# Banded attention of one layer: the softmax division moved from the weights to the output, with its sums on TensorE

## The reference, cut to what matters

```
def _pointwise(W, b, t):
    return jnp.einsum('oc,bct->bot', W, t) + b[None, :, None]
q, k, v = _pointwise(Wq, bq, x), _pointwise(Wk, bk, cond), _pointwise(Wv, bv, cond)
k, v = padded by 8 on the left and 7 on the right
k_win = k[:, :, idx].reshape(B, H, hd, T, W)
v_win = v[:, :, idx].reshape(B, H, hd, T, W)
dots = jnp.einsum('bhdt,bhdtw->bhtw', qh, k_win) * scale
attn = jax.nn.softmax(dots, axis=-1)
out = jnp.einsum('bhtw,bhdtw->bhdt', attn, v_win)
return _pointwise(Wo, bo, out.reshape(B, C, T))
```

## Time and profile before

| what | value |
|---|---|
| median of 3 runs | 2366.32 us (2362.61 to 2378.12) |
| the profiled execution, its own time | 2366.56 us |
| its span, first to last instruction | 2364.5 us |
| TensorE busy | 1939.2 us (82%) |
| VectorE busy | 1702.7 us (72%) |
| ScalarE busy | 559.1 us (24%) |
| GpSimd busy | 609.7 us (26%) |
| mean granted clock of TensorE | 0.894 |

### The profile page before, as it was taken

One profiled execution on the slowest core, in us unless ns is written; L12 is line 12 of the kernel. 1 busy time (PEld: TensorE's weight loads), 2 busy tenths in 40 slices (PEclk: granted clock), 3 DMA queues, 4 the chain that ended last, 5 costly groups with the idle time before them and its releaser, 6 DMA issues. The chain is left out here.

```text
span 2364.5 us, 40599 instructions
## 1 busy us (share of the span) xinstructions
PE 1939.2 (82%) x14722; PEld 1103.0 (47%) x14872; DVE 1702.7 (72%) x3005; ACT 559.1 (24%) x1326; POOL 609.7 (26%) x728
## 2 busy tenths in 40 slices
PE   4587879877898788887766798989899989898876
PEld 2343556435653455544543354545454545454432
DVE  4489655895459954698536788878788878887875
ACT  2221223222332223222221222222222222222221
POOL 0310213002230103201012434333334343434220
PEclk7699778997699986999857999999999999999987
DMA  7357202461043700453004212021212021200100
GB/s 228 134 139 202 63 2 82 125 188 54 1 127 111 204 8 1 131 158 106 1 18 142 72 28 62 28 61 27 63 28 62 27 62 27 62 27 27 31 24 36
DMA packets 134552, 176.08 MB, mean 74 GB/s; under 512 B 46304, under 2 KB 73568, under 8 KB 134288
## 3 DMA queue, kind: packets, MB, share of 16 engines
q1 hardware_dynamic: 134416, 174.20, 24.9%
HBM read 132.09 MB, written 42.07 MB: 74 GB/s over the span
## 5 line engine op out<-in xcount | busy, mean ns | idle before, releaser
L1122 POOL TENSOR_TENSOR early_vare<-early_mv,w_eps 128x1 f32<-128x1 f32 x96 | 31.3, 326 | 837.3 <-DVE early_mv L1187 823.0
L350 PE MATMUL la_ps<-w_xTl,la_wqh 128*128 128x512 bf16 x511 | 198.7, 389 | 13.5 <-POOL la_wql L2040 8.0
L2035 POOL TENSOR_TENSOR la_q<-la_straight,la_rot 128x512 f32<-128x512 f32 x128 | 164.2, 1283 | 175.3 <-DVE la_rot L2095 175.3
L350 PE MATMUL la_ps<-la_wol,la_oTh 128*128 128x512 bf16 x512 | 199.6, 390 | 6.2 <-issue 0.4
L349 PE MATMUL la_ps<-w_xTh,la_wqh 128*128 128x512 bf16 x504 | 197.6, 392 | 5.3 <-DVE la_rot L2095 4.6
L351 PE MATMUL la_ps<-la_woh,la_oTl 128*128 128x512 bf16 x511 | 198.2, 388 | 0.0
L351 PE MATMUL la_ps<-w_xTh,la_wql 128*128 128x512 bf16 x503 | 195.4, 388 | 0.1
L2048 POOL TENSOR_TENSOR la_p<-la_s,la_rec 128x256 f32<-128x256 f32 x128 | 92.9, 726 | 391.1 <-DVE la_rec L2116 390.5
L736 PE MATMUL early_ps<-early_products,w_heads 128*32 128x512 f32 x1024 | 132.1, 638 | 66.2 <-DVE early_products L1338 35.3
L349 PE MATMUL la_ps<-la_woh,la_oTh 128*128 128x512 bf16 x401 | 156.9, 391 | 10.8 <-DVE la_oTl L2123 9.1
L1939 ACT ACTIVATE la_s<-la_s 128x256 f32<-128x256 f32 x128 | 53.3, 417 | 421.4 <-DVE la_s L2109 421.4
(11 more groups left out here) (329 smaller groups left out, 4619.3 us busy)
## 6 DMA issues: line engine op xcount, KB each, us to landing
early_vR<-scr_v SPq DMA_DIRECT2D x128, 257.0 KB, 5.0
early_wkv<-wkv SPq DMA_DIRECT2D x32, 512.0 KB, 4.1
la_v<-v SPq DMA_DIRECT2D x64, 256.0 KB, 3.8
k<-early_ctxt SPq DMA_DIRECT2D x32, 256.0 KB, 3.6
v<-early_ctxt SPq DMA_DIRECT2D x64, 128.0 KB, 2.8
scr_p<-early_weights SPq DMA_DIRECT2D x16, 512.0 KB, 2.6
early_pR<-scr_p SPq DMA_DIRECT2D x32, 256.0 KB, 3.5
w_raw_q<-in_Wq SPq DMA_DIRECT2D x8, 1024.0 KB, 6.4
```

The source lines that it names most:

```text
L350: pe.matmul(out, lh[c], rl[c], start=False, stop=False)
L2035: rope_sum.send(pool.tensor_tensor(dst, straight[:, slot, :], rot[:, slot, :], ALU.add))
```

## The change

The exponentials are written by ScalarE straight into `turned`, undivided, and sent to DRAM from there. TensorE sums the 16 slices of `turned` with 16 float32 products by the identity, 64 columns each (`sum_weights`, into a new step `den1` of bank 0). VectorE takes the reciprocal of these 64 sums (`invert`, into the one tile `rec1`). SyncE writes `rec1` to a new DRAM tensor `scr_r` and reads it back with each head's row repeated on the eight partitions of the output layout, into one of two tiles `over` (`divisors`). VectorE multiplies the output sum by it (`divide`), which takes the place of ScalarE's `out_copy`. `over` shares memory with `rmix` and `hs`, which other stages use. `divide` of tile j-1 and `invert(3)` stand between the two halves of `times_values`; the last `divide` stands behind all of it. New waits: the maximum of tile j waits for the exponentials of tile j-1, ScalarE's exponentials for the sums and the DRAM copy of the tile before, `invert(j)` until `rec1` of tile j-1 is in DRAM.

```
@@ plan @@
+            plan += [(("den1", j), 0) for j in range(QUAD)]
@@ SyncE @@
             def weights_by_shift(turn, j):
-                p1_ready.wait(apart, turn, j)
+                exp1_ready.wait(apart, turn, j)
...
+            def divisors(turn, j):
+                rec1_ready.wait(apart, turn, j)
+                rec1_written.send(sp.dma_start(scr_r[j].rearrange("h c t -> c h t"), rec1[:, :]))
+                if j >= 2:
+                    banks.wait_drained(apart, turn, "sum1", j - 2)
+                rec1_written.wait(sp, turn, j)
+                src = scr_r[j, 0:1, 0, 0:1]
+                src = bass.AP(src.tensor, src.offset, [[0, CH], [TC * TP, HEADS], [1, D]])
+                over_in[j % 2].send(sp.dma_start(over[j % 2], src))
...
                 weights_by_shift(turn, 1)
+                divisors(turn, 0)
                 for f in range(6, 8):
                     keep_kv(turn, f)
                 shifted_values(turn, 2)
-                for f in range(8, 10):
-                    keep_kv(turn, f)
                 weights_by_shift(turn, 2)
-                for f in range(10, 12):
+                divisors(turn, 1)
+                for f in range(8, 12):
                     keep_kv(turn, f)
                 shifted_values(turn, 3)
+                divisors(turn, 2)
                 weights_by_shift(turn, 3)
-                for f in range(12, 2 * KV):
+                for f in range(12, 2 * KV - 1):
                     keep_kv(turn, f)
+                divisors(turn, 3)
+                keep_kv(turn, 2 * KV - 1)
@@ TensorE @@
+                def sum_weights(j):
+                    exp1_ready.wait(pe, turn, j)
+                    banks.wait_free(pe, turn, "den1", j)
+                    for k in range(WIN):
+                        last = pe.matmul(banks.bank("den1", j)[:, 0:TP], ident, turned[:, k, :],
+                                         start=(k == 0), stop=(k == WIN - 1))
+                    banks.fill(last, "den1", j)
...
                 queries_keys(3)
+                sum_weights(0)
                 last_keys_values(3, 4, 5)
                 sum_depth(2)
+                sum_weights(1)
                 last_keys_values(6, 7)
                 sum_window(0)
+                last_keys_values(8)
+                sum_depth(3)
+                sum_weights(2)
+                last_keys_values(9, 10, 11)
                 out_proj(0)
-                last_keys_values(8, 9)
-                sum_depth(3)
-                last_keys_values(10, 11)
                 sum_window(1)
+                sum_weights(3)
+                last_keys_values(12, 13, 14)
                 out_proj(1)
-                last_keys_values(12, 13, 14)
                 sum_window(2)
+                last_keys_values(15)
                 out_proj(2)
-                last_keys_values(15)
                 sum_window(3)
@@ ScalarE @@
             def exponentials1(turn, j):
...
-                exp1_ready.send(act.activation(ee[:, :, :], ee[:, :, :], ACT.Exp, scale=float(CH) ** -0.5))
+                if j >= 1:
+                    p1_written.wait(act, turn, j - 1)
+                    banks.wait_filled(act, turn, "den1", j - 1)
+                exp1_ready.send(act.activation(turned[:, :, :].rearrange("p w t -> p t w"), ee[:, :, :], ACT.Exp,
+                                               scale=float(CH) ** -0.5))
@@ VectorE @@
+                def invert(j):
+                    banks.wait_filled(dve, turn, "den1", j)
+                    if j >= 1:
+                        rec1_written.wait(dve, turn, j - 1)
+                    last = dve.reciprocal(rec1[:, :], banks.bank("den1", j)[:, 0:TP])
...
+                        if h == 0 and j == 2:
+                            invert(3)
+                        if h == 0 and j >= 1:
+                            divide(j - 1)
...
                 def divide(j):
-                    exp1_ready.wait(dve, turn, j)
-                    st.link(dve.tensor_reduce(sum1[:, :], ee[:, :, :], AX.X, ALU.add))
-                    st.link(dve.reciprocal(rec1[:, :], sum1[:, :]))
+                    over_in[j % 2].wait(dve, turn, j // 2)
+                    banks.wait_filled(dve, turn, "sum1", j)
                     if j >= 1:
-                        p1_written.wait(dve, turn, j - 1)
-                    p1_ready.send(dve.tensor_tensor(turned[:, :, :], ee[:, :, :].rearrange("p t w -> p w t"),
-                                                    rec1[:, :].unsqueeze(1).to_broadcast([P, WIN, TP]), ALU.mult))
+                        banks.wait_filled(dve, turn, "out1", j - 1)
+                    banks.drain(dve.tensor_tensor(oS[:, :], banks.bank("sum1", j), over[j % 2], ALU.mult),
+                                "sum1", j)
```

42 lines of the change are left out of this document (21 added, 21 removed).

## The result

The changed kernel takes 2427.5 us (median of 4, 2423.3 to 2437.4), the kernel before 2367.6 beside it: a ratio of 1.026, interval 1.023 to 1.029. It is 60 us slower; the forecast was 37. The profiled execution took 2423.3 us with a span of 2421.6.

What follows compares the result with a forecast made beforehand. VectorE was taken to bound layer 1's attention. Per turn 14.6 and 2.6 us go, 5.5 and waits of 22.4 come; 9.2 was taken, 36.8 over four turns, on 2366.6: 2403 us, range 2381 to 2428.

Steps and rivals of the forecast that it cites:

- the walk through turn 1: Attention of layer 1, turn 1: following VectorE, TensorE and SyncE through the new order gave waits of 22.4 us.
- the wait that decides: Last reciprocal, inside values 2: waits 7.8 us for tile 2's reciprocals to reach DRAM behind tile 3's value loads.
- the sign of being right: Attention of layer 1: it would take 107 to 110 us a turn.
- Where the bound lies: Attention of layer 1: VectorE bounds it, busy 94.4 of 98.5 us in turn 1, with TensorE and SyncE close beside.
- what goes and comes on VectorE: VectorE, each turn: old divides of 14.6 us go, new reciprocals and products of 5.5 us come.
- The price of a sum of weights: TensorE: the 16 float32 products of one sum take 3.4 us at the full clock.
- cheap sums: Rival on TensorE's sums of weights: products take 1.4 us, 4.7 less a turn, total 2384 us; chance 0.19.
- the rival of dear sums: TensorE's sums of weights: 5.1 us each adds 5.1 a turn, total 2424 us; chance 0.15.
- ScalarE at nothing: ScalarE loses its output copy and writes exponentials in strides; with slack all through the stage, costed at nothing.
- TensorE's lateness: VectorE waits for TensorE: 4.5 us before values 0, 1.3 before keys 3, 3.1 before values 2.
- The copy did not overtake: Rival on the reciprocals' write: it lands at 85.2 instead of 88.0, 2.8 us less a turn, total 2392; chance 0.06.
- The rival in which the gain comes through: Attention of layer 1: only VectorE's work counts, a turn nets -8.9 us, total 2331; chance 0.07.

Runs made afterwards that it cites:

- e8: Changed kernel with ScalarE writing its exponentials in the order it reads them instead of turned: 2432.9 us, ratio 1.027.
- e1: Changed kernel with the reciprocals of tile 2 ahead of the value loads of tile 3 in SyncE's queue: 2435.0 us, ratio 1.028.
- e2: Changed kernel with two tiles for the reciprocals, so the last reciprocal no longer waits for the write of tile 2's: 2428.9 us, ratio 1.025.
- e3: Changed kernel with two reciprocal tiles and, on SyncE, the weights of tile 3 ahead of the reciprocals of tile 2: 2414.9 us, ratio 1.019.
- e6: Changed kernel with reciprocals made but neither written to memory nor read back; a constant multiplies the output: 2401.7 us, ratio 1.015.
- e14: Changed kernel with divisors summed from weights read back from DRAM, inverted by ScalarE, SyncE's queue ordered by need, keys-and-values steps moved later: 2351.9 us, ratio 0.994.
- e4: Changed kernel with 15 of the 16 products of each sum of weights left out: 2430.5 us, ratio 1.025.
- e13: Changed kernel without the reciprocals' trip through memory and without 15 of 16 products of each sum: 2384.1 us, ratio 1.007.

## Why the prediction was right in kind and short in size

The step that failed is the sizing of the walk through turn 1, above all the step called the wait that decides. The sum had 22.4 us of waits there; the same waits came to 28.0. The wait before the last reciprocal was 10.5 for 7.8, since the value loads ahead of the write left at 82.3 for 77.8; the one before values 3 4.15 for 2.8, the one before the last divide 3.55 for 2.05. Two terms were taken as nothing and were not: the first depth sums, 1.5 more than before, and 0.8 for handing on four reciprocals. A turn took 112.7 to 116.7 us where 107 to 110 was given as the sign of being right.

- **Where the bound lies, and what goes and comes on VectorE:** right. It is busy 9.3 us less a turn; by the rows 14.6 went and 4.9 came, four times 0.55 and 0.68, so 9.7.
- **The price of a sum of weights:** right, 3.6 us for 3.4 at a granted clock of 1.00. The rivals of cheap sums (1.4, and 0.9 by the Trainium skill) and of dear ones (5.1) fall. That the rival of dear sums named 2424, nearer to the result than the forecast, is luck: it made the waits before values 0, keys 3 and values 2 grow by 1.7 each, and they did not. The rule of the Trainium skill on the load of weights (TensorE: Matmul & The Clock Gate, section on LDWEIGHTS) comes close here, 113 ns an instruction against 107. The Trainium skill's rule in VectorE: DVE Perf Modes, section on the TRN2 errata, would be 29 ns, an estimate worked out in the prediction, and doesn't hold for float32 products of this shape.
- **ScalarE at nothing:** the exponentials doubled, 2.04 us for 1.05, which I had not priced. In e8 the stage is no shorter without it, so no price shows above the scatter of 2 to 3 us a turn.
- **TensorE's lateness** before values 0 and keys 3: 4.9 and 1.2 for 4.5 and 1.3. Ahead of values 2 it is 2.9 in two waits for 3.1, of which 1.6 is released by the write of reciprocals and not by TensorE.
- **The order that decides:** right in place and kind; e1 to e3 and e6 bear it out. The copy did not overtake: it was in 10.7 us after the first load's issue, for 10.2 taken. The rival in which the gain comes through falls with it, since it wanted the reciprocals in DRAM within 2.5 us.
- **Where the sum was short,** in turn 1 (stage 116.5 for 108.6): (1) the loads of tile 3 start at 82.3, not 77.8. The value sums of tile 1 stood at 79.6, and SyncE then spent 2.7 us more on keeps and a weight load that stood ahead in its queue. I had let it start the moment its wait was over. (2) The weights of tile 3 took 5.1 us, not 3.4, and reached VectorE at 103.0 instead of 96.5, 1.5 more than was lost by then. (3) TensorE ran at the lower level of its clock where I had taken the upper one. The first depth sums cost 2.3, not 0.8, with a granted clock of 0.55 in their second half; the last value sums cost 3.6, not 2.05: 3.0. (4) A reciprocal with its hand-on is 0.9 us, not 0.67: 0.8. Of the queue's 2.7 and these three, 8.0, the turn's miss is made, to within 0.1. Over four turns the miss is 24: I had entered 9.2 a turn, turn 1 grew by 18.1, and the others, which had more waits to lose, by 14.4 on average.
- **Half clock at the first depth sums:** the kernel before waits 2.0 us there in one turn of four, the changed one 2.0 to 2.3 in three, e6 and e14 1.9 to 2.5 in three, e3 2.4 to 2.5 in two. No run settles whether the change brings it or chance does.
- **Other stages:** right for the kernel itself, 1960 us for 1965, though that is closer than one profile can tell: this time spreads by 21 us over runs that are alike there.

## What to carry to other kernels

When an intermediate is handed over through memory, price what it stands behind and what then stands behind it in the issuing queue, not its bytes: here transfers of 32 KB, four a turn, cost 29 us in four turns. Before fixing the longest wait, ask which chain ends last there; removing the wait on `scr_r` by itself gave 1 us a turn, while the same queue ordered by need, with the trip gone, gave a kernel faster than both, in the stage by more than all the waits that VectorE had there before. A step that looks like filler may carry a load inside it: move it only with the list of what waits for that load.

## What the runs showed that I had not expected

- ScalarE writes 128x1024 float32 with a stride of 256 bytes in 2.04 us, in order in 1.06.
- GpSimd's power of a 128x512 tile takes 82 to 86 us, while its addition of that size takes 1.3. VectorE's reciprocal grows by 6.25 ns an element: 0.55 us for 64, 3.35 for 512.
- Where VectorE waits for its own reciprocal before it announces it to SyncE, the next instruction starts 0.3 us after the reciprocal's end; in e6, which does not announce, it starts without that gap.
- Time outside the stage spreads from 1960 to 1981 us over the profiles of the changed kernel, e1 to e4, e6 and e13, which are alike there. Of 29 us saved in the stage e6 shows 24 in its total, e4 2 of its 12.
